# A transformer tower in one kernel: attention's input normalised inside the dense experts, query and key maxima from an unpadded product, attention three steps behind, switch-expert weights split earlier

## Chip, cores and metric

The kernel runs on one core of one Trainium2 chip. The metric is the device time of one execution in microseconds (us). Several executions are timed and their median is given. One further execution is recorded by the hardware profiler, and all rows below come from that one. TensorE is PE in the rows, its weight loads are PEld, VectorE is DVE, ScalarE is ACT, GpSimd is POOL, and SyncE's DMA queue is SPq.

## What is computed

The input is x of 16 x 2048 tokens of width 192 (D). A score keeps some of the tokens. Then four blocks follow, each adding to the stream h:

```python
h = _L0_tok_ref(x, ...)
h = h + _L0_attn_ref(_layernorm(h), ...)     # a state space scan
h = h + _L0_ffn_ref(_layernorm(h), ...)      # 16 dense experts and a shared one
h = h + _L1_attn_ref(_layernorm(h), ...)     # attention, 12 heads of 16, 8-bit fake_quant
h = h + _L1_ffn_ref(_layernorm(h), ...)      # 16 switch experts, 64 slots each in a batch
```

What matters here is the third line from below and the next one. `fake_quant` needs the largest absolute value of a whole tensor before it can round any of it:

```python
def fake_quant(x, n_bits=N_BITS):
    scale = jnp.maximum(jnp.max(jnp.abs(x)) / qmax, 1e-08)
    q = jnp.clip(jnp.round(x / scale), -qmax - 1, qmax) * scale
qkv = jnp.einsum('bnc,oc->bno', fake_quant(x), fake_quant(w_qkv)) + b_qkv
attn = jnp.einsum('bhnd,bhmd->bhnm', fake_quant(q), fake_quant(k)) * scale
out = jnp.einsum('bhnm,bhmd->bhnd', fake_quant(softmax(attn)), fake_quant(v))
out = jnp.einsum('bnc,oc->bno', fake_quant(out), fake_quant(w_proj)) + b_proj
```

So attention's input, q, k, v and its output each force a pass that only finds a maximum, with a result of one number for the whole chip, before the pass that uses it.

## The kernel before

The program is a row of stages. Every stage is a block of its own with buffers of its own; a block ends when all engines and its stores are done, so nothing overlaps across a seam. Names of buffers begin with the letter of their stage.

- a (token selection) and b (state space scan) are not touched.
- cw loads the dense experts' weights in five pieces; ACT writes the high part of each (line 842) and DVE the low part (line 849).
- c, in `dense_experts`, runs over NC = 20 chunks of 420 rows (four tiles of 105). A chunk has 17 slots e, one for an expert. In each slot PE makes up and gate products (`c_pU`, `c_pG`, lines 1032 to 1034), ACT the silu `c_su` (1118), DVE `c_pG` (1246) and `c_ac` (1253), ACT the high part `c_ap` (1121), POOL the low part (976), and PE the down product `c_pD` (1041). DVE fits the next chunk's routing into slots 4 to 12 and a row statistic into slots 0, 1, 2 and 12 (`STAT_AT`); ACT normalises in slots 13 to 16. At the end of a chunk `finish` adds `c_pD` to `c_y` (line 1223) and SP stores `c_y` (924) as h2.
- d, the first part of `attention_inputs`, loads h2 again, 16 batches of 525 rows (five tiles of 105), takes row statistics on DVE (1284 to 1292), normalises on ACT (1394), takes the maximum (1421, 1423) and stores `xn`. Behind the batches it quantises and transposes the attention weights (1430 to 1470) and lays them out with each head of 16 padded to 32 rows (`wT`).
- e loads xn by batch, rounds it (1606, 1610), transposes it (PE 1547, ACT 1584 to `e_xT`), multiplies it with the padded weights in six groups of 128 columns (PE 1560), copies each group out on ACT (`e_y`, 1591) and takes its maximum on DVE (1619), then v in two groups (PE 1567, DVE `e_vb` 1628) with its maximum (1637) and three small steps that merge the maxima (1640 to 1643). No q or k is kept; only the maxima, v and the transposed input are.
- f makes q and k once more, now scaled and rounded. g finds the softmax's row maxima and sums. It also fills the switch experts' slot table with zeros (`dram_slots`, line 1855, 16 DMAs of `k_empty`), which n later scatters into.
- h multiplies the probabilities with v. A batch has TN = 17 steps n of three 128 x 512 tiles. PE fills `h_pS` for step n+1 (`fill`, 2101, 2105); ACT takes the exponent into `h_ex` (2189); DVE rounds it into `h_pr` (2260); PE combines it with v into `h_pO` (`combine`, 2119, 2122), two steps behind. `h_ex`, `h_pr` and `h_pS` have two buffers, `h_pO` one. After the last tile of each of three groups of heads (steps 5, 11 and 16) DVE copies `h_pO` out (`evacuate`, 2228, at DVE's n = 7, 13 and 1 of the next batch) before PE may write the next group; `largest` (2237, 2239) takes its maximum.
- i is the output projection. n is the router, which scatters rows into slots (POOL, 2504).
- o, in `switch_experts`, runs 16 experts, each with four chunks of 256 slots: PE transposes (2773, 2774), `o_pH` (2789 to 2791) and `o_pY` (2800, 2803). The weights of the next expert are split while the current one runs: high parts on ACT (2828 to 2830), low parts on POOL (2864, 2865) and a narrow rest on DVE (2906). POOL also scatters the results (`out_dram`, 2875, two for each chunk, waiting for DVE's `o_yr`).

The order of instructions on each engine is the order in which the code is written. An engine runs its own list in order and waits at a semaphore; `at(b, n, d)` is the count after b rounds of n signals and d more.

## Time and profile before

| | us |
|---|---|
| median of three runs | 4838.54 |
| lowest and highest | 4837.43, 4840.34 |
| the profiled execution | 4844.94 |
| its span | 4843.2 |
| c, first product's wait to last result | 1194 to 2418.65 |
| d, first load to last copy | 2422.96 to 2547.1 |
| e | 2548.07 to about 2724 |
| f | about 2728 to 2827 |
| g | 2833 to 3419.8 |
| h | 3421.38 to 3929.3 |
| i | 3931.82 to about 4049 |
| n | 4051.70 to about 4280 |
| o | 4283.33 to the end |

The profiled execution took 4844.94 us, of which 4843.2 are its span. A group's row names the line, the engine, the operation, what it writes and reads, and how many instructions stand together; times are the start and the length. In square brackets stands how long the engine had been idle and what released it. Between about 1 and 10 us pass at each seam in which no engine computes.

### The profile page before, as it was taken

Reading aid. Unit: us, or ns where it says so; the run is one execution under the profiler, and the core shown is the slowest. Engines: PE = TensorE matmul, PEld = TensorE weight load, DVE = VectorE, ACT = ScalarE, POOL = GpSimd, SP = SyncE. Lnnn points to the kernel's source line nnn. Section 1 sums busy time; section 2 is a strip of 40 time slices with the busy share of each in tenths; the row PEclk is TensorE's granted clock in tenths of the full one; section 3 lists DMA queues with packets and bytes.
Section 4 is the critical chain, followed back from the end, with each engine's and each line's share of the span. In section 5 each row is a group of like instructions: output and inputs, shape, how many; then the busy total and the mean of one; then the engine's idle time right before and its main releaser. Section 6 shows DMA issues by size and latency. Waiting matters only on the chain. (4 is left out here: it accounts for less than half of the span.)

```text
span 4843.2 us, 75411 instructions
## 1 busy us (share of the span) xinstructions
PE 3765.6 (78%) x23732; PEld 2846.5 (59%) x23732; DVE 3528.1 (73%) x6651; ACT 2607.0 (54%) x5078; POOL 1768.2 (37%) x2215
## 2 busy tenths in 40 slices
PE   0059999995899999999907778888788853559998
PEld 0049999994799999999904421111122223459998
DVE  6849888986666666666477669999677755856665
ACT  4535555553344444444334579999788842433332
POOL 4647777773244444433300012222100012433333
PEclk9999999997899999999955655555555555579999
DMA  3235555444222222222233590000111145443332
GB/s 96 84 90 149 140 135 147 138 134 117 78 78 78 78 78 78 78 78 76 75 112 91 169 343 30 22 22 23 63 67 67 66 133 143 126 123 95 116 117 69
DMA packets 285815, 484.45 MB, mean 100 GB/s; under 512 B 47214, under 2 KB 217134, under 8 KB 272594
## 3 DMA queue, kind: packets, MB, share of 16 engines
q1 hardware_dynamic: 264082, 455.22, 30.4%
q0 software_dynamic: 20480, 25.87, 1.8%
q8 instruction: 115, 1.88, 0.2%
q14 instruction: 114, 0.93, 0.1%
q10 hardware_dynamic: 1024, 0.54, 0.0%
HBM read 354.05 MB, written 136.51 MB: 101 GB/s over the span
## 5 line engine op out<-in xcount | busy, mean ns | idle before, releaser
L976 POOL TENSOR_TENSOR c_ap<-c_ac,c_ap 128x420 fp32r<-128x420 f32 x340 | 428.6, 1261 | 733.9 <-ACT c_ap L1121 733.5
L693 PE MATMUL b_pA<-b_woutT,b_ys 128*105 128x192 f32 x3840 | 689.4, 326 | 1.3 <-ACT b_ho L579 0.4
L693 PEld LDWEIGHTS b_pA<-b_woutT,b_ys 128*105 128x105 f32 x3840 | 610.5, 171 | 12.1 <-ACT b_ho L579 3.9
L491 POOL TENSOR_TENSOR b_ys<-b_hs,b_cb 128x525 f32<-128x525 f32 x384 | 507.4, 1322 | 221.1 <-DVE b_hs L776 178.2
L1953 DVE TENSOR_REDUCE g_raw<-g_pS 128x1 f32<-128x525 f32 x816 | 549.5, 703 | 31.0 <-PE g_pS L1908 29.7
L1929 ACT ACTIVATE g_pS<-g_pS,g_stt 128x525 f32<-128x525 f32 x816 | 553.7, 776 | 19.3 <-POOL g_stt L1882 18.5
L1908 PE MATMUL g_pS<-g_qk 16*128 16x262 bf16 (+1 forms) x1536 | 461.4, 408 | 93.2 <-ACT g_pS L1929 35.7
L776 DVE TENSOR_TENSOR_SCAN b_hs<-b_ae,b_pB 128x525 f32<-128x525 f32 x384 | 479.1, 1248 | 39.8 <-ACT b_ae L606 5.1
L1121 ACT ACTIVATE c_ap<-c_ac 128x420 fp32r<-128x420 f32 x340 | 189.2, 557 | 589.9 <-DVE c_ac L1253 588.2
L1246 DVE SCALAR_TENSOR_TENSOR c_pG<-c_pG,c_bc,c_su 128x420 f32<-128x420 f32 x340 | 225.5, 663 | 325.1 <-ACT c_su L1118 316.8
L1041 PE MATMUL c_pD<-cw_wd,c_ap 128*105 128x192 f32 x4080 | 438.6, 257 | 18.6 <-POOL c_ap L976 18.6
L1041 PEld LDWEIGHTS c_pD<-cw_wd,c_ap 128*105 128x105 f32 x4080 | 424.3, 172 | 42.5 <-POOL c_ap L976 29.5
L2189 ACT ACTIVATE h_ex<-h_pS 128x1536 f32<-128x1536 f32 x272 | 385.3, 1451 | 85.2 <-DVE h_pr L2260 70.0
L1908 PEld LDWEIGHTS g_pS<-g_qk 16*128 16x128 bf16 x1536 | 95.5, 106 | 459.2 <-ACT g_pS L1929 425.9
L2260 DVE TENSOR_SCALAR h_pr<-h_ex 128x1536 bf16<-128x1536 f32 x272 | 257.6, 961 | 102.2 <-PE h_pO L2119 59.0
L606 ACT ACTIVATE b_ae<-b_delta,b_nlam 128x525 f32<-128x525 f32 x384 | 270.6, 727 | 82.0 <-DVE b_hs L776 79.6
L1882 POOL TENSOR_TENSOR g_stt<-g_raw,k_cs 128x1 f32<-128x1 f32 x816 | 155.9, 191 | 405.4 <-DVE g_raw L1953 405.4
L1032 PE MATMUL c_pU<-c_xp,cw_wu 128*128 128x420 f32 x1020 | 269.2, 372 | 28.3 <-DVE c_ac L1253 28.3
L767 DVE TENSOR_TENSOR b_pB<-b_delta,b_pB 128x525 f32<-128x525 f32 x384 | 265.3, 691 | 31.1 <-PE b_pB L683 29.2
L1929 ACT ACTIVATION_READ_ACCUMULATOR g_pS<-g_pS,g_stt 128x1 f32 x816 | 253.7, 311 | 0.0
L2875 POOL DMA_INDIRECT out_dram<-o_yr,o_xr x128 | 125.0, 977 | 346.6 <-DVE o_yr L2929 325.2
L1032 PE MATMUL c_pG<-c_xp,cw_wg 128*128 128x420 f32 x1020 | 250.7, 354 | 0.0
(385 smaller groups left out, 8366.6 us busy)
## 6 DMA issues: line engine op xcount, KB each, us to landing
b_cb<-dram_ct SPq DMA_DIRECT2D x64, 1050.0 KB
c_wb<-dram_wt SPq DMA_DIRECT2D x60, 840.0 KB, 10.5
b_cb<-dram_ct SPq DMA_DIRECT2D x64, 525.0 KB
dram_slots<-k_empty SPq DMA_DIRECT2D x16, 1544.0 KB
...
```

Source lines behind the costliest of these rows:

```text
L491: pool.tensor_tensor(ys[:, u % RING, :], hs[:, u % RING, :], cb[:, g % 3, u % GU, :], ALU.mult).then_inc(s["ys"], 1)
L606: act.activation(ae[:, u % RING, :], delta[:, k, q, :], ACT.Exp, scale=nlam[:, u:u + 1])\
L693: ins = pe.matmul(into, ys[:, u % RING, t * TP:(t + 1) * TP], woutT[:, u % NU, :], start=(u == 0 and t % 2 == 0), stop=(u % NU == NU - 1), ...
L767: v.tensor_tensor(pB[:, u % 2, OFF:OFF + S], delta[:, k, 0 if u < NS else 1, :], pB[:, u % 2, OFF:OFF + S], ALU.mult).then_inc(s["bm"], 1)
L776: v.tensor_tensor_scan(hs[:, u % RING, :], ae[:, u % RING, :], pB[:, u % 2, OFF:OFF + S], 0.0, ALU.mult, ALU.add).then_inc(s["hs"], 1)
L976: nc.gpsimd.tensor_tensor(ap[LO][:, r, :], ac[:, r, :], ap[HI][:, r, :].bitcast(F32), ALU.subtract)\
L1032: pe.matmul(into, ws[b][:, e, :], xp[a][:, k, 0, :], start=(n == 0), stop=False)
L1041: ins = pe.matmul(pD[:, t // 2, (t % 2) * D:(t % 2 + 1) * D], ap[a][:, (e + k) % 2, t * TP:(t + 1) * TP], wd_s[b][:, e, :], start=False, s ...
L1908: ins = pe.matmul(pS[:, slot, OFF + lo:OFF + hi], mine, qk[at_, k, 3 + g, lo:hi], start=True, stop=True)
L1929: nc.scalar.activation(x, x, ACT.Exp, bias=stt[:, k, 0, c:c + 1], scale=cs, accum_out=stt[:, k, 1, c:c + 1]).then_inc(s["exp"], 1)
L1953: v.tensor_reduce(raw[:, k, c:c + 1], pS[:, q % RING, OFF:OFF + S], AX, ALU.max, negate=True)\
L2189: nc.scalar.activation(ex[:, (n + k) % 2, :], pS[:, (n + k) % 2, :, :].rearrange("p t l -> p (t l)"), ACT.Exp, scale=cs).then_inc(s["E"], 1)
```

## The change

Five parts.

1. Stage d is gone. Its weight work (maxima, rounding, 18 transposes, copies, bias loads) now stands in the cw block, between the five `low_part` steps of DVE, with one more layout without padding (`wcT`) and its bias (`bc`). Its work on rows is in c: statistics of the finished chunk c-1 on DVE in slots 3, 13, 14 and 15, the normalisation of chunk c-2 on ACT in slots 6 to 9, its maximum on DVE in slot 16, and a second store (`store_normed`) on SP. `c_y` has three buffers. What is left of chunks 18 and 19, and the global maximum, follow the last chunk.
2. Stage e multiplies with the unpadded weights: three groups instead of six, so 12 products instead of 24, three copies and three maxima. Maxima of a batch go to columns of `e_mq` and `e_mv` and are merged once at the end. PE transposes the next batch ahead of v. It is written out for all batches, with three buffers of `e_y`.
3. The zero fill of the slot table is made from a buffer of half the size in g itself: 32 DMAs of 772 KB instead of 16 of 1544 KB, behind a wait for POOL's memset.
4. Stage h combines three steps behind, with three `h_ex` and four `h_pr`; DVE copies out at n = 8, 14 and 2; `largest` writes a column of `h_om`, and one reduction ends the stage. It is written out.
5. The first switch expert's weights are loaded at the start of n and split at its end. In o, POOL makes the low parts of the next expert's weights before it waits for the chunk's `o_yr`, no longer after its two scatters.

```diff
+    OSTAT_AT, OLN_AT, OMAX_AT = {3: 0, 13: 1, 14: 2, 15: 3}, {6: 0, 7: 1, 8: 2, 9: 3}, 16
...
+            sp.dma_start(wq_n[:, :, :], w_qkv.rearrange("(r p) c -> p r c", p=KC)).then_inc(s_wq, 16)
+            sp.dma_start(wp_n[:, :, :], w_proj.rearrange("(r p) c -> p r c", p=KC)).then_inc(s_wq, 16)
...
+            dve.wait_ge(s_wq, 32)
+            v.tensor_reduce(K["amax"][0:KC, 1:2], wq_n[:, :, :].rearrange("p r c -> p (r c)"), AX, ALU.max,
+                            apply_absolute_value=True).then_inc(s_m0, 1)
+            v.tensor_reduce(K["amax"][0:KC, 2:3], wp_n[:, :, :].rearrange("p r c -> p (r c)"), AX, ALU.max,
+                            apply_absolute_value=True).then_inc(s_m0, 1)
+            low_part(0)
+            st = Steps(dve, s_v2)
+            dve.wait_ge(s_all, 1)
+            quant_scale(nc, st, K["sc"][:, 1:3], K["inv"][:, 1:3], K["gmax"][:, 1:3])
...
+            dve.sem_inc(s_tc, 1)
+            low_part(1)
+            for c in range(KT):
+                dve.wait_ge(s_t, c + 1)
+                for r in range(4):
+                    v.tensor_copy(K["wT"][:, c, r * 6 * HP:(r + 1) * 6 * HP].rearrange("p (h d) -> p h d", d=HP)[:, :, 0:HD],
+                                  pT[0:KC, c, r * KC:(r + 1) * KC].rearrange("p (h d) -> p h d", d=HD))
+                v.tensor_copy(K["wcT"][:, c, :], pT[0:KC, c, 0:4 * KC])
+                ins = v.tensor_copy(K["wvT"][:, c, :], pT[0:KC, c, 4 * KC:6 * KC])
+            ins.then_inc(s_tc, 1)
+            low_part(2)
+            dve.wait_ge(s_t, 3)
...
+            def store_normed(c):
+                sp.wait_ge(s["zn"], at(c, 1, 1))
+                sp.dma_start(xn_d[c * CT:(c + 1) * CT, :, :].rearrange("t p d -> p t d"), z[:, c % 2, :, :])\
+                    .then_inc(s_z[c % 2], 16)
 
             def body(c, i, k, last):
                 rows(c + 3)
-                sp.wait_ge(s_out[k], i * 16)
-                sp.dma_start(y[:, k, :, :], tiles(h1, c)).then_inc(s_y[k], 16)
+                if c >= YR:
+                    sp.wait_ge(s_out[c % YR], c // YR * 16)
+                    sp.wait_ge(s["zn"], at(c - YR, 1, 1))
+                sp.dma_start(y[:, c % YR, :, :], tiles(h1, c)).then_inc(s_y[c % YR], 16)
                 if last < 2:
                     weights(c + 1, range(len(GROUPS)))
-                store(c, k)
+                if c >= 2:
+                    store_normed(c - 2)
+                store(c)
 
...
+        def normalise_result(c, t):
+            act = nc.scalar
+            if t == 0:
+                act.wait_ge(s["ostat"], at(c, 1, 1))
+                act.wait_ge(s["zm"], at(c, 1, -1))
+                act.wait_ge(s_z[c % 2], c // 2 * 16)
+            ins = act.activation(z[:, c % 2, t, :], y[:, c % YR, t, :], ACT.Identity, bias=nb2[:, t:t + 1],
+                                 scale=rs2[:, t:t + 1])
+            if t == CT - 1:
+                ins.then_inc(s["zn"], 1)
...
+                    if c >= 1:
+                        if e == min(OSTAT_AT):
+                            so = Steps(dve, s_vo, VP, c - 1)
+                        if e in OSTAT_AT:
+                            result_statistics(c - 1, OSTAT_AT[e], so)
+                    if c >= 2 and e == OMAX_AT:
+                        result_largest(c - 2)
                 finish(c, i, k)
 
             written_out(NC, body)
...
+            so = Steps(dve, s_vo, VP, NC - 1)
+            for part in range(4):
+                result_statistics(NC - 1, part, so)
+            for c in (NC - 2, NC - 1):
+                result_largest(c)
+            dve.wait_ge(s["zm"], at(NC - 1, 1, 1))
+            v.tensor_reduce(K["amax"][0:TP, 0:1], zm[:, :], AX, ALU.max).then_inc(s_m0, 1)
+            dve.wait_ge(s_all, 1)
...
+                for r in range(3):
+                    pe.wait_ge(s["y"], at(b, 3, r - 2))
+                    if r < 2:
+                        pe.wait_ge(s["vb"], at(b, 2, r - 1))
+                    for lo, hi in CUT:
+                        for c in range(KT):
+                            ins = pe.matmul(pQ[:, r, OFF + lo:OFF + hi], K["wcT"][:, c, r * 128:(r + 1) * 128],
+                                            xT[:, k, c, lo:hi], start=(c == 0), stop=(c == KT - 1))
+                    ins.then_inc(s["qk"], 1)
+                if last < 2:
+                    transposes(b + 1, 1 - k)
+                for r, (lo, hi) in enumerate(KV):
+                    pe.wait_ge(s["y"], at(b, 3, r + 1))
...
+            def body(b, i, k, last):
+                for r in range(3):
+                    act.wait_ge(s["qk"], at(b, 3, r + 1))
+                    act.wait_ge(s["max"], at(b, 3, r - 2))
+                    nc.scalar.activation(y[:, r, :], pQ[:, r, OFF:OFF + S], ACT.Identity,
+                                         bias=K["bc"][:, r:r + 1], scale=K["cq"][:, 0:1]).then_inc(s["y"], 1)
+                if last < 2:
+                    columns(b + 1, i + k, 1 - k)
+
...
+                for r in range(3):
+                    dve.wait_ge(s["y"], at(b, 3, r + 1))
+                    v.tensor_reduce(mq[:, r, b:b + 1], y[:, r, :], AX, ALU.max,
+                                    apply_absolute_value=True).then_inc(s["max"], 1)
+                dve.wait_ge(s_o2[k], i * 16)
+                dve.wait_ge(s["vmax"], at(b, 1, -1))
+                if last == 0:
+                    integers(b + 2, i + 1, k)
+                for r, (lo, hi) in enumerate(KV):
...
-SW, ER = 2 * D + 2, 8
+SW, ER = 2 * D + 2, 4
...
+            sp.wait_ge(s_i, 6)
...
-        ex = sb("ex", [128, 2, 3 * QM])
-        pr = sb("pr", [128, 2, 3 * QM], BF16)
+        BEHIND, EXR, PRR = 3, 3, 4
+        ex = sb("ex", [128, EXR, 3 * QM])
+        pr = sb("pr", [128, PRR, 3 * QM], BF16)
...
-        om = sb("om", [128, 1])
+        om = sb("om", [128, NB * HG])
...
-                    if n >= 2:
-                        combine(b, i, k, n - 2)
+                    if n >= BEHIND:
+                        combine(b, i, k, n - BEHIND)
                     elif not first:
-                        combine(b - 1, i + k - 1, 1 - k, TN + n - 2)
...
-                    act.wait_ge(s["P"], at(b, TN, n - 1))
-                    nc.scalar.activation(ex[:, (n + k) % 2, :], pS[:, (n + k) % 2, :, :].rearrange("p t l -> p (t l)"),
+                    act.wait_ge(s["P"], at(b, TN, n + 1 - EXR))
...
-                v.tensor_reduce(om[:, :], oT[:, k, g, :], AX, ALU.max, apply_absolute_value=True).then_inc(s_om, 1)
-                dve.wait_ge(s_om, b * HG + (g + 1))
-                v.tensor_tensor(K["amax"][:, 7:8], K["amax"][:, 7:8], om[:, :], ALU.max).then_inc(s["om"], 1)
-                dve.wait_ge(s["om"], at(b, HG, g + 1))
+                c = b * HG + g
+                v.tensor_reduce(om[:, c:c + 1], oT[:, k, g, :], AX, ALU.max, apply_absolute_value=True)\
+                    .then_inc(s["om"], 1)
...
-                    if n == 1 and not first:
+                    if n == BEHIND - 1 and not first:
                         evacuate(b - 1, i + k - 1, 1 - k, 2)
-                    if n in (7, 13):
-                        evacuate(b, i, k, 0 if n == 7 else 1)
+                    if n in (5 + BEHIND, 11 + BEHIND):
+                        evacuate(b, i, k, 0 if n == 5 + BEHIND else 1)
                     dve.wait_ge(s["E"], at(b, TN, n + 1))
-                    wait_combined(dve, b, n - 2)
-                    v.tensor_scalar(pr[:, (n + k) % 2, :], ex[:, (n + k) % 2, :], MAGIC, -MAGIC, ALU.add, ALU.add)\
+                    if n >= PRR or not first:
+                        wait_combined(dve, b, n - PRR)
+                    v.tensor_scalar(pr[:, (b * TN + n) % PRR, :], ex[:, (b * TN + n) % EXR, :], MAGIC, -MAGIC, ALU.add,
...
+                load_weights(sp, 0)
...
+                low_parts(pool, 0, 0)
...
+                high_parts(act, 0, 0)
...
-                split_weights(0, 0)
 
                 def body(c, i, j, last):
+                    if j % CE == 1 and not (last and j > CE):
+                        low_parts(pool, i * 2 + (j // CE + 1), 1 - j // CE)
                     pool.wait_ge(s["y"], at(c, 1, 1))
                     pool.sem_inc(s_go, 1)
                     for t in range(CT):
                         pool.indirect_dma_start(out.rearrange("b s d -> (b s) d"), bass.IndirectOffsetOnAxis(
                             ap=xr[:, j, t, PT:PT + 1].bitcast(U32), axis=0), yr[:, j % 4, t, :], None,
                             bounds_check=last_row, oob_is_err=False).then_inc(s_y[j % 4], 16)
-                    if j % CE == 1 and not (last and j > CE):
-                        split_weights(i * 2 + (j // CE + 1), 1 - j // CE)
 ```

DVE in e, one batch near the end of the stage. `k_amax` and `e_mt` merge the maxima. Before:

```order
L1619 TENSOR_REDUCE e_mtq<-e_y 128x1 x3
L1606 TENSOR_SCALAR e_xr<-e_x,k_inv 105x960
L1610 TENSOR_SCALAR e_xb<-e_xr 105x960
L1619 TENSOR_REDUCE e_mtq<-e_y 128x1 x3
L1628 SCALAR_TENSOR_TENSOR e_vb<-e_pQ,k_cq,k_bv 105x384 x2
L1628 SCALAR_TENSOR_TENSOR e_vb<-e_pQ,k_cq,k_bv 105x192
L1637 TENSOR_REDUCE e_mt<-e_vb 105x1
L1640 TENSOR_REDUCE e_mt<-e_mtq 128x2
L1642 TENSOR_TENSOR k_amax<-k_amax,e_mt 128x2
L1643 TENSOR_TENSOR k_amax<-k_amax,e_mt 105x1
```

And the same engine and place after the change:

```order
L1613 TENSOR_REDUCE e_mq<-e_y 128x1 x3
L1601 TENSOR_SCALAR e_xr<-e_x,k_inv 105x960
L1605 TENSOR_SCALAR e_xb<-e_xr 105x960
L1624 SCALAR_TENSOR_TENSOR e_vb<-e_pQ,k_cq,k_bv 105x384 x2
L1624 SCALAR_TENSOR_TENSOR e_vb<-e_pQ,k_cq,k_bv 105x192
L1630 TENSOR_REDUCE e_mv<-e_vb 105x1
```

Three reductions of a group and the three merging steps are gone from each batch.

DVE in h around the copy-out of the second group of heads (`h_oT<-h_pO`). Before:

```order
L2260 TENSOR_SCALAR h_pr<-h_ex 128x1536 x3
L2232 COPY h_oT<-h_pR 128x13
L2228 COPY h_oT<-h_pO 128x512
L2260 TENSOR_SCALAR h_pr<-h_ex 128x1536 x2
L2222 TENSOR_TENSOR h_qk<-h_qk,h_pR 128x525
```

And after:

```order
L2270 TENSOR_SCALAR h_pr<-h_ex 128x1536 x3
L2242 COPY h_oT<-h_pR 128x13
L2270 TENSOR_SCALAR h_pr<-h_ex 128x1536
L2236 COPY h_oT<-h_pO 128x512
L2270 TENSOR_SCALAR h_pr<-h_ex 128x1536
L2230 TENSOR_TENSOR h_qk<-h_qk,h_pR 128x525
```

The copy-out stands one rounding step later.

POOL in o, at the second chunk of an expert. Before:

```order
L2875 DMA out_dram<-o_yr,o_xr 8400x192 x2
L2863 ISA
L2864 TENSOR_TENSOR o_wi<-o_wi_r,o_wi 128x768
L2865 TENSOR_TENSOR o_wo<-o_wo_r,o_wo 128x6x192
L2872 REGISTER_ALU
L2875 DMA out_dram<-o_yr,o_xr 8400x192 x2
```

And after:

```order
L2899 DMA out_dram<-o_yr,o_xr 8400x192 x2
L2456 ISA
L2457 TENSOR_TENSOR m_wi<-m_wi_r,m_wi 128x768
L2458 TENSOR_TENSOR m_wo<-m_wo_r,m_wo 128x6x192
L2896 REGISTER_ALU
L2899 DMA out_dram<-o_yr,o_xr 8400x192 x2
```

The rows read alike, but the scatters above the two splits are those of the second chunk before and those of the first chunk after, since a scatter pair has moved from above to below.

## Rows read from the trace of the kernel before

**Rows 1.** Windows: stretch, its length, busy us (instructions) by engine, PEclk, DMA share, GB/s

```profile
1500.00:1600.00 100.00, 95.61 (x681) 91.36 (x680) 71.85 (x134) 41.50 (x77) 42.00 (x34) 1.00 0.23 78
...
2548.00:2724.00 176.00, 140.92 (x704) 83.37 (x704) 132.88 (x238) 93.45 (x128) 0.00 (x0) 0.50 0.31 90
...
3535.00:3635.00 100.00, 84.89 (x626) 22.71 (x626) 75.73 (x128) 80.64 (x67) 2.81 (x6) 0.50 0.20 69
```

**Rows 2.** Timeline at the seams from c to d to e: start, length, instruction

```profile
2417.63 1.02 DVE L1223 TENSOR_TENSOR c_y<-c_pD,c_y 105x384 f32<-105x384 f32 x2 [3.18 <-PE c_pD L1041]
...
2422.96 0.32 SPq L1336 DMA_DIRECT2D d_wq_n<-in_L_attn_w_qkv_dram  x1
...
2548.07 4.91 SPq L1508 DMA_DIRECT2D e_x<-dram_xn  x3
```

**Rows 3.** Timeline of DVE, the first row statistic of stage c

```profile
1200.80 1.14 DVE L1141 BATCH_NORM_STATS2 c_stats<-c_h 105x6 f32<-105x192 f32 x4 [7.13 <-DMA c_bd_s<-in_L_ffn_sbd_dram]
...
1204.88 0.16 DVE L1157 SCALAR_TENSOR_TENSOR c_nb<-c_mv,c_rs 105x4 f32<-105x4 f32 x1
```

**Rows 4.** Timeline of ACT in the weight block cw

```profile
1182.23 2.02 ACT L842 ACTIVATE cw_wgt<-cw_raw 128x2176 fp32r<-128x2176 f32 x1 [3.17 <-DMA cw_raw<-in_L_ffn_sWg_dram]
```

**Rows 5.** Stage c: timeline of DVE; then waits of 1500:2300 (us in total, times, longest)

```profile
1603.85 1.06 DVE L1150 TENSOR_SCALAR c_rs<-c_hh 105x4 int32<-105x4 int32 x1
...
PE c_pU L1032 <- DVE c_ac L1253: 17.9, 29, 1.0
```

**Rows 6.** Timeline of ACT, PE and DVE over one batch of stage e

```profile
2575.75 1.10 ACT L1584 ACTIVATE e_xT<-e_pT 96x525 bf16<-96x525 bf16 x2 [1.96 <-PE e_pT L1547]
...
2586.19 1.10 ACT L1584 ACTIVATE e_xT<-e_pT 96x525 bf16<-96x525 bf16 x2 [1.63 <-PE e_pT L1547]
...
2577.08 5.97 PE L1560 MATMUL e_pQ<-e_xT,k_wT 96*128 96x263 bf16 x24 [1.52 <-ACT e_xT L1584]
...
2579.08 0.70 DVE L1619 TENSOR_REDUCE e_mtq<-e_y 128x1 f32<-128x525 f32 x1 [1.28 <-ACT e_y L1591]
...
2585.20 1.46 DVE L1628 SCALAR_TENSOR_TENSOR e_vb<-e_pQ,k_cq,k_bv 105x384 f32<-105x384 f32 x3
2586.81 1.15 DVE L1637 TENSOR_REDUCE e_mt<-e_vb 105x1 f32<-105x960 f32 x1 [0.15 <-DVE e_vb L1628]
```

**Rows 7.** Stage h: timeline of POOL, once a batch; then waits of 3480:3900

```profile
3621.54 0.45 POOL L1794 TENSOR_TENSOR h_kt<-h_qk,h_mask 128x156 bf16<-128x156 bf16 x1 [4.07 <-DMA h_qk<-dram_qk]
...
3652.21 0.46 POOL L1794 TENSOR_TENSOR h_kt<-h_qk,h_mask 128x156 bf16<-128x156 bf16 x1 [4.01 <-DMA h_qk<-dram_qk]
...
ACT h_ex L2189 <- DVE h_pr L2260: 61.4, 81, 1.6
...
DVE h_pr L2260 <- PE h_pO L2119: 50.9, 67, 1.1
...
PE h_pO L2119 <- DVE h_oT L2228: 34.7, 42, 1.1
```

**Rows 8.** Timeline of ACT and POOL at the start of stage o

```profile
4292.97 0.84 ACT L2828 ACTIVATE o_wi<-o_wi_r 128x768 fp32r<-128x768 f32 x1 [30.16 <-DMA o_wo_r<-in_L_ffn_wo_dram]
...
4298.21 2.61 POOL L2865 TENSOR_TENSOR o_wo<-o_wo_r,o_wo 128x1152 fp32r<-128x1152 f32 x1
```

**Rows 9.** Timeline of DVE, ACT and PE around an expert's first product in o

```profile
4295.63 0.95 DVE L2906 TENSOR_TENSOR o_wi_t<-o_wi_r,o_wi_t 64x768 fp32r<-64x768 f32 x1 [27.42 <-ACT o_wo L2830]
...
4393.63 4.61 DVE L2906 TENSOR_TENSOR o_wi_t<-o_wi_r,o_wi_t 64x768 fp32r<-64x768 f32 x1
...
4386.81 1.16 ACT L2830 ACTIVATE o_wo<-o_wo_r 128x1152 fp32r<-128x1152 f32 x1
...
4398.44 0.61 PE L2789 MATMUL o_pH<-o_xT,o_wi 128*128 128x256 f32 x3 [2.35 <-issue]
...
4399.28 0.84 PE L2789 MATMUL o_pH<-o_xT,o_wi 128*128 128x256 f32 x3
...
4403.01 0.52 PE L2789 MATMUL o_pH<-o_xT,o_wi 128*128 128x256 f32 x3
```

## What the change was expected to do

> **What bounds the kernel now.** The stages run one after the other, so each has to be read alone. First the busy time by windows [rows 1]. In c PE is busy 95.61 of 100 us at full clock, DVE 71.85. In e PE is busy 140.92 of 176 us and DVE 132.88, at clock 0.50: two engines that hand work to each other. In h PE is busy 84.89 of 100 us, ACT 80.64, DVE 75.73, at 0.50: nobody is full. Then the timeline at the seams, which shows d as a stage in which PE has nearly nothing to do [rows 2]. Then the waits and timelines of e, h and o, for what ends the idle time there. The sum is made against the profiled execution's 4844.94 us; the median of the three runs is 4838.54, 6.4 us less, and I take these 6.4 off at the end.
>
> **Stage d goes.** The last result of c is written at 2417.63 + 1.02 = 2418.65, and e's first load is issued at 2548.07 [rows 2]: 129.4 us. After the change this stretch holds only a tail. Statistics of the last chunk cost what they cost at the start of c, where DVE is alone: 1200.80 to 1205.04 [rows 3], 4.2 us. Four ACT normalisations of 105x192 come next; I estimate 2 us. The maximum over 105x768 is about 768/960 of the 1.15 us reduction of 105x960 [rows 6], 0.9 us, but runs beside the store's flight. From c's last result to the first load of d, store and seam took 2422.96 - 2418.65 = 4.3 us [rows 2]; the same comes behind the store of the normalised rows, with about 1.5 us for the last reduction, the one over partitions and the scale. 4.2 + 2 + 4.3 + 1.5 = 12 us. **Saved: 117**, bounds 110 to 121.
>
> **The weight work in cw.** DVE gets about 8 us more in five gaps, and ACT and DVE wait there for DMA: 3.17 us before the fourth piece [rows 4]. Most fits. The two new loads (576 KB) stand first in the queue and push the pieces back; the fourth wait shows that a piece arrives every 5.2 us for 1.1 MB, so about 2.7 us. **+3**, bounds 1 and 8.
>
> **The row work in c.** Each chunk gets on DVE the 4.2 us of a statistic [rows 3], and 0.9 of a maximum; on ACT four normalisations; on SP one wait and one store behind the next chunk's weights and ahead of the store of h2. 20 x 5.1 = 102 us of DVE work lie beside PE, since DVE is idle 28 of 100 us [rows 1], 16 in a chunk of about 59, and the slots chosen carry no routing. What it costs is delay, not work. Small DVE steps are sometimes held while POOL runs: a step on a few elements took 0.16 us alone [rows 3] and 1.06 here [rows 5]. This is the place to weigh a rule: the Trainium skill, page "SBUF — State Buffer", section "SBUF: two separate sides", says that POOL and a DVE instruction with two SBUF inputs or in a fast mode take one pair of ports as an exclusive lock, and the later one waits for the whole other instruction. The rows agree in kind; by that rule all new steps may each be held, and also hold POOL's `c_ap`.
> PE waits for `c_ac` at each chunk's start, 17.9 us in 29 waits over 800 us [rows 5], so a late DVE at the end of slot 16 goes straight to PE. The new maximum stands just there. Slots 13 to 16 get about 1.2 us each where, at 16 us in 17 slots, they have some 1 to 2 us idle. I take 0.3 us a chunk: **+6**, bounds 0 and 24 (1.2 us a chunk, one held step that nothing absorbs). If the cover were gone altogether it would be 102.
>
> **Stage e.** A batch takes 2586.19 - 2575.75 = 10.44 us [rows 6]: 24 products in 5.97 us, then v, while ACT and DVE follow with six copies and six maxima. PE's busy time a batch is 140.92 / 16 = 8.8 us, less twelve products of 0.25: 5.8. DVE's is 132.88 / 16 = 8.3 [rows 1], less three maxima of 0.70 and three merging steps of 0.16: 5.7. The loop that closes runs from `e_vb` to the first maximum of the next batch, since `e_pQ` is shared: from the first product to that maximum it was 2579.08 - 2577.08 = 2.0 us [rows 6], plus 0.2 for the signal. DVE has the rest of `e_vb` (0.5) and the maximum of v (1.15) to do in it, so 0.6 is idle; its steps that follow each other with a wait cost some 0.8 more. 5.7 + 0.6 + 0.8 = 7.1. The transposes, ahead of v now, hide the 1.52 us in which PE waits for `e_xT` [rows 6]. 16 x (10.44 - 7.15) = **-52**, bounds -40 (8 us, if the loop shows one more wait) and -62 (6.6, DVE gapless).
>
> **Stages f and g.** f is not touched. In g the zero fill is the same bytes in twice the DMAs, now behind a memset; nobody reads the table until n. 0, bounds -8 and +3.
>
> **Stage h.** A batch takes 3652.21 - 3621.54 = 30.67 us [rows 7]. ACT waits for DVE's rounding (61.4 us in 81 waits over 420 us, 13.7 batches), DVE for PE's `combine` (50.9 in 67), PE for the copy-out (34.7 in 42) [rows 7]. The first two are buffers: `h_ex` and `h_pr` have two each. With three and four, and a combine one step later, both go. The third stays, for `h_pO` still has one buffer: three times 0.8 us a batch. Then PE is next: 84.89% of 30.67 is 26.0 us [rows 1], plus 3 x 0.8 = 2.4, is 28.4; ACT needs 80.64%, 24.7. DVE loses 48 merging steps. Saved 2.3 x 16 = 37, and a little in the written-out loop. **-38**, bounds -15 (the steps around each copy-out still drain two engines) and -50 (the copy-out partly hidden as well).
>
> **Start of o.** The first weights reach ACT at 4292.97, and POOL ends its split at 4298.21 + 2.61 = 4300.82, when PE may start [rows 8]. Now they are split already and PE needs only its rows: some 10 us less. Against it POOL's 5.2 us of splits stand behind n's last scatters and may hold the seam. **-8**, bounds -11 and 0.
>
> **The stalls in o.** At each new expert PE waits 2.35 us [rows 9]; the row says "issue", but the start, 4398.44, follows the end of DVE's step 2906 at 4398.24, which took 4.61 us where the first of its kind took 0.95 [rows 9]. It was held while POOL split the same weights. After the change POOL splits right after ACT's high parts, which ended at 4386.81 + 1.16 = 4387.97 [rows 9], and POOL's two splits take twice 2.6 us [rows 8], so until about 4393.2. DVE's step at 4393.63 is then free and done at 4394.6, before PE needs it at 4398.44 - 2.35 = 4396.1. 15 experts after the first: 15 x 2.3 = 34. Behind each stall PE runs at half clock: groups of three products take 0.84 us where they later take 0.52 [rows 9], four groups of 1.0 in place of 0.59, 1.6 us lost, x15 = 24. I take 21 of it. **-55**, bounds -27 and -60.
>
> Sum: -117 + 3 + 6 - 52 + 0 - 38 - 8 - 55 = -261. 4844.94 - 261 = 4583.9 profiled, 4577.5 as the median.
>
> **Rivals.**
> 1. h stays coupled: around the copy-out PE, DVE and ACT drain as now, and the longer buffers only move the waits. For it: 42 PE waits on the copy-out are untouched, and it is one DVE step later. Against: two of the three waits are plain buffer waits. Gain 15 in place of 38: 4600.5.
> 2. The clock rises in h and e. h would have fewer gaps on PE than now, and c, which has few, runs at 2.4 GHz where h runs at 1.2 [rows 1]. ACT then bounds h at 24.7 + 0.3: 3.4 x 16 = 54 more, and e goes to 6.5, 10 more: 4513.5. Against: the three copy-outs a batch stay as gaps, and no stretch of h is above 0.50 so far. The Trainium skill, "TensorE: Matmul & The Clock Gate", Part 1, says that activity lifts the clock from 1.2 to 2.4 GHz; by it the rival is the likelier the fewer gaps are left. h's row at 0.50 shows only how it is with the gaps of now [rows 1].
> 3. The stall in o only moves: POOL's splits are slowed by DVE, end after 4393.6, and DVE's step is held by the second of them or by the scatters. Half of the 55 stays: 4604.5.
> 4. c pays 1.2 us a chunk, +24 in place of +6: 4595.5.
> 5. e does not shorten as walked (the 8 us batch, and v's wait for ACT's copies ahead of it): +14 to +25: 4597.
> 6. **The slower side**, one mechanism: in c the held small steps delay `c_ac` in slots 13 to 16, POOL's `c_ap` follows late, PE empties, and the delay repeats in each chunk. It decides from (261 + 6) / 20 = 13.4 us a chunk, over a fifth of one: with 14 the median is 4577.5 + 20 x 14 - 6 = 4851.5. DVE's idle 16 us in a chunk against 5.1 speak against it.
> That the change does nothing is no case: d's loads and batches are gone from the program.
>
> **How the numbers follow.** Forecast 0.50; rival 1 0.13; rival 2 0.11; rival 3 0.12; rival 4 0.08; rival 5 0.04; rival 6 and failures like it 0.02. The forecast's own bounds add to about 4565 to 4595. For 8 in 10 the range takes in rivals 1, 3, 4 and 5, two of them together, and the clock rising in e alone or for a part of h: 4540 to 4622. About 0.2% (9.7 us) is what a measurement can tell: faster by more 0.975, within 0.010, slower 0.015, all from rival 6 and its approach.
>
> **What would show it.** c ends where it did, within 10 us, plus 3 for cw. From c's last `c_y` to e's first load 12 us. e's `e_xT` every 7.1 us. h's `h_kt` every 28.4 us, with no wait of DVE for PE's combine and PE's waits on `h_oT` left. In o no idle before an expert's first product, DVE's narrow step at 0.95 us, and PE's clock at 1.00. Wrong would be: `c_pU` waiting over 2 us for `c_ac`, a clock other than 0.50 in h, or a DVE step of over 2 us in o.

## The result and the profile after

The kernel before took 4839.44 in four runs beside it (4837.43 to 4843.04). The ratio is 0.9523, with a 95% interval of 0.9506 to 0.9539. The forecast was 4577.5, with a range of 4540 to 4622. So the sign and the range hold, and the gain of 231 us is 30 less than the 261 that the sum gave. The kernels of the experiments below ran once each, except the last one (`best`). Their stage times come from that one profile, so a difference is held against the spread of stages whose code is the same; the last section lists it.

The profiled execution took 4606.7 us, of a span of 4605.0. The stages, each from its first DMA issue to that of the next one, in us:

| stage | before | after | difference | forecast |
|---|---|---|---|---|
| cw, c, d (to e's first load) | 1387.1 | 1283.1 | -104.0 | -108 |
| e | 180.3 | 142.2 | -38.1 | -52 |
| f | 105.2 | 103.1 | -2.1 | 0 |
| g | 587.9 | 587.9 | 0.0 | 0 |
| h | 510.4 | 476.3 | -34.1 | -38 |
| i | 119.9 | 120.6 | +0.7 | 0 |
| n | 231.6 | 238.3 | +6.7 | with o |
| o | 559.9 | 492.9 | -67.0 | -63 with n |

In the profiled executions the difference is 4844.94 - 4606.7 = 238.2 us, against 261. The windows of the changed kernel answer to [rows 1]; the columns are the same:

```profile
1500.00:1600.00 100.00, 94.53 (x679) 90.40 (x678) 79.06 (x168) 47.48 (x87) 41.93 (x33) 1.00 0.18 61
...
2452.00:2575.00 123.00, 76.43 (x478) 61.35 (x476) 87.22 (x132) 51.97 (x75) 0.00 (x0) 0.59 0.41 114
...
3400.00:3500.00 100.00, 85.14 (x649) 24.33 (x659) 79.77 (x130) 84.24 (x71) 6.91 (x8) 0.50 0.22 76
...
4200.00:4300.00 100.00, 100.00 (x785) 100.00 (x784) 60.48 (x113) 40.44 (x65) 45.77 (x36) 1.00 0.36 109
```

In o's window PE is never idle now and its clock is 1.00. In h the busy share of PE is as it was, 85%, over shorter batches. In e PE is busy 76.43 of 123 us, 62%, where it was 80% [rows 1]: it does less work and waits more.

The seam from c to e, which answers to [rows 2], in the timeline of DVE and SP:

```profile
2431.92 1.02 DVE L1382 TENSOR_TENSOR c_y<-c_pD,c_y 105x384 f32<-105x384 f32 x2 [1.66 <-PE c_pD L1154]
...
2433.35 5.99 SPq L1025 DMA_DIRECT2D dram_xn<-c_z  x2
2443.63 0.85 SPq L1494 DMA_DIRECT2D e_x<-dram_xn  x2
```

From 2432.94 to 2443.63 are 10.7 us in place of 129.4.

### The profile page after: what moved, and what is told of

Same layout as the page of the kernel before. It is cut to its first block and busy times, and to the rows that moved or that the text cites. A ratio compares the mean times of both kernels' runs of the same rounds, so it can differ in the third digit from the quotient of the medians.

```text
span 4605.0 us, 72550 instructions
## 1 busy us (share of the span) xinstructions
PE 3655.4 (79%) x23492; PEld 2806.7 (61%) x23540; DVE 3458.5 (75%) x6558; ACT 2558.1 (56%) x5030; POOL 1784.9 (39%) x2216
## 5 line engine op out<-in xcount | busy, mean ns | idle before, releaser
L1086 POOL TENSOR_TENSOR c_ap<-c_ac,c_ap 128x420 fp32r<-128x420 f32 x340 | 428.2, 1260 | 743.8 <-ACT c_ap L1245 743.4
L1154 PE MATMUL c_pD<-cw_wd,c_ap 128*105 128x192 f32 x4080 | 438.1, 257 | 27.5 <-POOL c_ap L1086 27.5
L1154 PEld LDWEIGHTS c_pD<-cw_wd,c_ap 128*105 128x105 f32 x4080 | 423.6, 172 | 51.5 <-POOL c_ap L1086 38.4
L2197 ACT ACTIVATE h_ex<-h_pS 128x1536 f32<-128x1536 f32 x272 | 374.7, 1465 | 48.9 <-PE h_pS L2109 27.5
L1405 DVE SCALAR_TENSOR_TENSOR c_pG<-c_pG,c_bc,c_su 128x420 f32<-128x420 f32 x340 | 225.4, 663 | 228.0 <-ACT c_su L1242 218.6
L2270 DVE TENSOR_SCALAR h_pr<-h_ex 128x1536 bf16<-128x1536 f32 x272 | 259.1, 962 | 68.7 <-ACT h_ex L2197 56.2
L1145 PE MATMUL c_pU<-c_xp,cw_wu 128*128 128x420 f32 x1020 | 268.4, 371 | 30.4 <-DVE c_ac L1412 30.4
L1145 PE MATMUL c_pG<-c_xp,cw_wg 128*128 128x420 f32 x1020 | 251.3, 355 | 0.0
L2899 POOL DMA_INDIRECT out_dram<-o_yr,o_xr x128 | 132.1, 1032 | 261.3 <-DVE o_yr L2945 237.7
```

What stands on the lines that cost most here:

```text
L1086: nc.gpsimd.tensor_tensor(ap[LO][:, r, :], ac[:, r, :], ap[HI][:, r, :].bitcast(F32), ALU.subtract)\
L1145: pe.matmul(into, ws[b][:, e, :], xp[a][:, k, 0, :], start=(n == 0), stop=False)
L1154: ins = pe.matmul(pD[:, t // 2, (t % 2) * D:(t % 2 + 1) * D], ap[a][:, (e + k) % 2, t * TP:(t + 1) * TP], wd_s[b][:, e, :], start=False, s ...
L2197: nc.scalar.activation(ex[:, (b * TN + n) % EXR, :], pS[:, (n + k) % 2, :, :].rearrange("p t l -> p (t l)"), ACT.Exp, scale=cs).then_inc(s ...
```

## Stage e: where the largest miss was

The waits of e in the changed kernel (us in total, times, longest; 2450 to 2580), and one batch in the timeline of SP, DVE and PE:

```profile
PE e_pQ L1548 <- DVE e_vb L1624: 46.8, 15, 4.3
DVE e_xr L1601 <- DMA e_x<-dram_xn: 20.6, 13, 2.4
...
2483.69 0.35 SPq L1494 DMA_DIRECT2D e_x<-dram_xn  x1
...
2489.52 0.72 DVE L1601 TENSOR_SCALAR e_xr<-e_x,k_inv 105x960 f32<-105x960 f32 x1 [2.19 <-DMA e_x<-dram_xn]
...
2490.85 1.46 DVE L1624 SCALAR_TENSOR_TENSOR e_vb<-e_pQ,k_cq,k_bv 105x384 f32<-105x384 f32 x3
...
2492.13 2.79 PE L1548 MATMUL e_pQ<-e_xT,k_wcT 96*128 96x263 bf16 x12 [3.96 <-DVE e_vb L1624]
```

The load of `e_x` is issued at 2483.69 and DVE can round it only at 2489.52, 5.8 us later. DVE waits 2.19 us for it, with `e_vb` queued behind, and PE waits 3.96 us for `e_vb`. A batch takes 8.2 to 9.4 us where the walk gave 7.15. The theory: SP issues the load too late. Its buffer is free long before, but on SP it stands behind the store of v of the batch before, which waits for `e_vb`. The rival: the loop over `e_vb`, product, copy and maximum takes 8 us by itself.

**Load one batch earlier** (e_load).

```diff
-            for k in range(2):
-                load(k, 0, k)
+            for b in range(3):
+                load(b, b // 2, b % 2)
...
-                if not last:
-                    load(b + 2, i + 1, k)
+                if b + 3 < NB:
+                    load(b + 3, (b + 3) // 2, (b + 3) % 2)
```

> The changed kernel with SP issuing the load of e_x three batches ahead of the batch in work in place of two; buffers stay two. Theory (load late): e missed its forecast because DVE waits for e_x (20.6 us in 13 waits) with e_vb queued behind the rounding, and PE waits for e_vb. The wait goes, a batch takes 7.1 to 7.4 us where it takes 8.2 to 9.1, and e goes from 142 to 126 to 129 us. Rival (loop): the loop over e_vb, product, copy and maximum takes 8 us by itself; then DVE's wait for DMA moves to another wait and e stays over 138 us.

Measured: e 120.4 us in place of 142.2, the execution 4585.67. PE and DVE of that kernel:

```profile
2491.52 2.79 PE L1548 MATMUL e_pQ<-e_xT,k_wcT 96*128 96x263 bf16 x12 [1.60 <-DVE e_vb L1624]
...
2498.39 2.79 PE L1548 MATMUL e_pQ<-e_xT,k_wcT 96*128 96x263 bf16 x12 [1.59 <-DVE e_vb L1624]
...
2495.78 0.71 DVE L1601 TENSOR_SCALAR e_xr<-e_x,k_inv 105x960 f32<-105x960 f32 x1
```

The batch is 6.87 us and DVE's rounding waits for nothing. The load was the cause; e came out below the 126 to 129 us that were expected, so the rest of the walk was even a little too long.

**Rounding behind `e_vb`** (e_ints): the two steps of `integers(b + 2)` on DVE follow the maximum of v; the loads are issued as in the change.

```diff
-                if last == 0:
-                    integers(b + 2, i + 1, k)
                 for r, (lo, hi) in enumerate(KV):
...
                                 apply_absolute_value=True).then_inc(s["vmax"], 1)
+                if last == 0:
+                    integers(b + 2, i + 1, k)
```

> The changed kernel with DVE's rounding of batch b+2 (integers) behind e_vb and the maximum of v, in place of ahead of e_vb; loads as in the change. Theory (load late): e_vb no longer stands behind the wait for e_x, so PE's wait for e_vb (46.8 us in 15) falls under 20 us and e takes 126 to 133 us. Rival (loop): e stays over 138 us.

Measured: e 117.3 us, the execution 4586.13, with c 3 us longer in that run. It confirms the same from the other side: the loads are issued where they were, but the rounding comes later, finds its data and no longer stands in front of `e_vb`. e is 25 us shorter, again below the expectation, and a batch takes 6.57 us, less than the 6.87 of the early load. PE's rows tell where the 0.3 us are: the wait for `e_vb` is 1.10 us in place of 1.60.

```profile
2498.49 2.79 PE L1548 MATMUL e_pQ<-e_xT,k_wcT 96*128 96x263 bf16 x12 [1.10 <-DVE e_vb L1622]
```

What the halved products, the copies and the order of the transposes are worth one by one was not measured.

## Stage h: which of the three loosenings counts

In the changed kernel `h_kt` follows after 28.3 us in the two rows shown (POOL, answering to [rows 7]); twelve batches in the middle take 28.6 us in the mean, 26.6 to 30.1 each, where before they took 30.5. Among the waits of 3340 to 3700 DVE's for PE has nearly gone, and PE's for the copy-out has grown to 40.2 / 38 = 1.06 us each:

```profile
3407.30 0.45 POOL L1801 TENSOR_TENSOR h_kt<-h_qk,h_mask 128x156 bf16<-128x156 bf16 x1 [3.72 <-DMA h_qk<-dram_qk]
...
3435.64 0.46 POOL L1801 TENSOR_TENSOR h_kt<-h_qk,h_mask 128x156 bf16<-128x156 bf16 x1 [3.37 <-DMA h_qk<-dram_qk]
...
PE h_pO L2127 <- DVE h_oT L2236: 40.2, 38, 1.3
...
ACT h_ex L2197 <- PE h_pS L2109: 16.8, 25, 1.1
...
DVE h_pr L2270 <- PE h_pO L2127: 9.9, 26, 0.4
```

Three things were loosened together, and the maxima and the loop were changed too. All five runs edit the changed kernel. Four of them change only the numbers of this line (the copy-outs follow BEHIND), shown for h_lag2; h_om puts back the three lines of the maxima instead.

```diff
-        BEHIND, EXR, PRR = 3, 3, 4
+        BEHIND, EXR, PRR = 2, 3, 4
```

> The changed kernel with h combining two steps behind again (copy-outs at DVE n = 7, 13, 1), while h_ex keeps three and h_pr four buffers. Theory (buffers): the waits of ACT and DVE were for buffers, so most of h's gain stays: a batch takes 28.6 to 29.3 us (28.6 with the change, 30.7 before). Rival (lag): PE must be a step later for its rounding to be ready, and the batch goes back to 30 us or more, with PE waiting for h_pr.

> The changed kernel with two h_ex buffers in place of three; three steps behind and four h_pr stay. If ACT's wait for DVE (61.4 us over 420 before) was what the gain of h came from, it returns and a batch takes 29.5 to 30.7 us. If the gain is the lag and the buffers of h_pr, a batch stays at 28.6 to 29.0 us.

With a lag of two (2, 3, 4) h takes 475.0 us; with two `h_ex` (3, 2, 4) 476.3; the change has 476.3. Kernels with the same code of h spread over 2.1 us, so neither of the two is shown to be worth anything while the others stay. So everything was undone (2, 2, 2), and apart from that the maxima:

> The changed kernel with h two steps behind and two buffers each of h_ex and h_pr, so all of the looser order undone; the columns of maxima and the written-out order stay. h took 510.4 us before and 476.3 with the change; with either the lag or the third h_ex alone undone it took 475.0 and 476.3. Theory (h_pr): the number of h_pr buffers is what frees DVE and ACT; then h goes to 500 us or more. Rival (maxima): the gain is the 48 merging steps with their waits between DVE and itself; then h stays under 482 us.

> The changed kernel with only the maxima of h undone: one column, a TENSOR_TENSOR and two waits of DVE after each of 48 reductions, as before. Rival (maxima): h goes to 500 us or more. Theory (h_pr): 48 steps of about 0.4 us mostly hidden, h stays under 484 us.

Measured: (2, 2, 2) gives 501.7, the maxima undone alone 476.7. So 25.4 of the 34.1 us come from the three, and the 0.4 of the maxima, while the buffers are there, is inside the spread. The waits of (2, 2, 2), 3330 to 3700, are those of before again:

```profile
ACT h_ex L2197 <- DVE h_pr L2270: 48.3, 62, 1.6
...
DVE h_pr L2270 <- PE h_pO L2127: 44.3, 50, 1.1
```

Since each of two could stand in for the other, the last run keeps four `h_pr` and nothing else (2, 2, 4):

> The changed kernel with h two steps behind and two h_ex buffers as before; only h_pr keeps four. With all three undone h took 501.7 us, with the change 476.3; the lag alone undone gave 475.0, the third h_ex alone 476.3. Theory (h_pr alone): the copy-out of h_pO holds combine, and only more rounded tiles let DVE and ACT go on meanwhile; h stays under 480 us. Rival (any two): each of the lag and the third h_ex can stand in for the other, and one is needed; then h is 488 us or more.

Measured: 474.8 us. The execution took 4617.56, with the stages ahead of h longer than in the change. Here are the waits of that kernel, 3330 to 3700:

```profile
DVE h_pr L2270 <- ACT h_ex L2197: 48.9, 78, 0.9
...
PE h_pO L2127 <- DVE h_oT L2236: 32.9, 39, 1.1
...
ACT h_ex L2197 <- DVE h_pr L2270: 18.0, 13, 1.6
...
DVE h_pr L2270 <- PE h_pO L2127: 9.9, 26, 0.4
```

Two more buffers of `h_pr` are enough for all of it. The chain before was: PE waits for the copy-out of `h_pO`; so no `combine` frees an `h_pr`; DVE waits for that; so no `h_ex` comes free; ACT waits for that. With four `h_pr` DVE goes on rounding over the copy-out, and ACT waits for a free `h_ex` only once a batch (13 waits in 370 us, where (2, 2, 2) has 62). Whether a third `h_ex` with two `h_pr` would do the same was not run: four `h_pr` are shown to be enough, not to be the only cure. What remains open are 510.4 - 501.7 = 8.7 us: the order written out and the maxima, both still changed in (2, 2, 2), were not separated there.

## Stage c: half a microsecond in a chunk

A chunk took 59.20 us in the middle before and 59.89 after; from the first `c_y` to the last it was 1116.7 and is 1128.6. PE's waits, 1500 to 2300, show that the wait for POOL grew from 12.5 us and the one for `c_ac` [rows 5] hardly did; the DVE steps of the last chunk show why:

```profile
PE c_pD L1154 <- POOL c_ap L1086: 19.1, 27, 1.4
PE c_pU L1145 <- DVE c_ac L1412: 18.8, 28, 1.0
...
2423.05 1.05 DVE L1303 TENSOR_SCALAR c_rs<-c_hh 105x4 int32<-105x4 int32 x1
...
2426.14 1.08 DVE L1320 SCALAR_TENSOR_TENSOR c_hh<-c_hh,c_ve 105x4 f32<-105x4 f32 x1
...
2427.45 0.66 DVE L1405 SCALAR_TENSOR_TENSOR c_pG<-c_pG,c_bc,c_su 128x420 f32<-128x420 f32 x1
```

In slots 13 and 14 one small step each takes about 1 us in place of 0.16, and the next `c_pG` starts with no idle time before it, so DVE is late. Of the 13 new small steps of a chunk these two are the only ones held, and POOL's `c_ap` takes 1.27 us in the mean before and after. So the case that the prediction weighed, every new step held and `c_ap` with them, did not come. By offsets from `c_y` (mean of 12 chunks, against before), `c_ac` falls back by 0.44 us over slot 14. Theory: the two Newton steps of slot 14. Rival: the maximum in slot 16.

**One Newton step a slot** (c_newton):

```diff
-    OSTAT_AT, OLN_AT, OMAX_AT = {3: 0, 13: 1, 14: 2, 15: 3}, {6: 0, 7: 1, 8: 2, 9: 3}, 16
+    OSTAT_AT, OLN_AT, OMAX_AT = {3: 0, 13: 1, 14: 2, 15: 3, 16: 4}, {6: 0, 7: 1, 8: 2, 9: 3}, 16
...
-            elif part == 2:
-                newton(st, y_, v_, h_)
+            elif part < 4:
                 newton(st, y_, v_, h_)
```

> The changed kernel with the three Newton steps of the result's statistics spread over slots 14, 15 and 16 of c, one each, in place of two in slot 14 and one in 15; the maximum stays in slot 16. A chunk takes 59.9 us with the change and 59.2 before; PE's added wait is for c_ap at a chunk's end. Theory (slot 14): six small steps, one of them held while POOL runs, make DVE late in slot 14; spread, a chunk takes 59.3 to 59.6 and c is 5 to 11 us shorter. Rival (maximum): the maximum in slot 16 is what delays; no change, within 2 us.

**The maximum in slot 3 of the next chunk** (c_max3):

```diff
-                    if c >= 2 and e == OMAX_AT:
-                        result_largest(c - 2)
+                    if c >= 3 and e == OMAX_AT:
+                        result_largest(c - 3)
```

> The changed kernel with the maximum of the normalised rows moved from slot 16 to slot 3 of the next chunk. Theory (slot 14): no change of c, within 2 us. Rival (maximum): a chunk takes 59.3 to 59.6 us and c is 5 to 11 us shorter.

| | first to last `c_y` | middle chunk | `c_pD` waits for POOL, 1500:2300 |
|---|---|---|---|
| before | 1116.7 | 59.20 | 12.5 |
| change | 1128.6 | 59.89 | 19.1 |
| c_newton | 1125.5 | 59.68 | 14.0 |
| c_max3 | 1127.2 | 59.78 | 19.1 |
| both (in `best`) | 1120.3 | 59.36 | 14.0 |

Nine other kernels with c as in the change have 1128.6 to 1129.9, so 3 us is a difference and 1.4 is little more than their spread. Slot 14 is shown as the cause of PE's longer wait for POOL. Neither expectation of 5 to 11 us came: in c_newton one step fewer is held in a chunk, but the step that moved lands in front of the maximum in slot 16, and 0.25 us are lost there. With the maximum away as well 8.3 of the 11.9 us come back, more than the 3.1 and 1.4 of the two moves alone. So the theory and the rival each held a part of the cause, and 3.6 us stay open.

## Stage o, and the end of n

**The order of POOL undone** (o_order):

```diff
-                    if j % CE == 1 and not (last and j > CE):
-                        low_parts(pool, i * 2 + (j // CE + 1), 1 - j // CE)
                     pool.wait_ge(s["y"], at(c, 1, 1))
...
                             bounds_check=last_row, oob_is_err=False).then_inc(s_y[j % 4], 16)
+                    if j % CE == 1 and not (last and j > CE):
+                        low_parts(pool, i * 2 + (j // CE + 1), 1 - j // CE)
```

> The changed kernel with one part undone: in o POOL makes the low parts of the next expert's weights behind the second chunk's two scatters again, as before. Theory (order): the whole gain of o comes from this order. PE stalls about 2.3 us before each of 15 experts' first product, the DVE step on the narrow part (L2464) takes over 4 us in place of 0.95, PE runs at half clock after each stall, and o grows from 493 by 50 to 58 us. Rival (preload): the gain comes from the weights of the first expert and from loads that are issued earlier; then o grows by under 15 us.

Measured: 4669.08 us; o 549.9 in place of 492.9, so 57.0 us for this one order. PE's waits before the 15 first products sum to 34.6 us, which leaves 22.4; they are put down to PE's clock, as the windows further down show it. DVE and PE of that kernel, then POOL and DVE of the changed one at the same place:

```profile
4218.61 4.61 DVE L2464 TENSOR_TENSOR m_wi_t<-m_wi_r,m_wi_t 64x768 fp32r<-64x768 f32 x1
...
4223.43 0.62 PE L2825 MATMUL o_pH<-o_xT,m_wi 128*128 128x256 f32 x3 [2.35 <-issue]
```

```profile
4169.11 1.84 POOL L2457 TENSOR_TENSOR m_wi<-m_wi_r,m_wi 128x768 fp32r<-128x768 f32 x1 [2.52 <-ACT m_wo L2453]
4170.90 2.67 POOL L2458 TENSOR_TENSOR m_wo<-m_wo_r,m_wo 128x1152 fp32r<-128x1152 f32 x1
...
4174.68 0.95 DVE L2464 TENSOR_TENSOR m_wi_t<-m_wi_r,m_wi_t 64x768 fp32r<-64x768 f32 x1
```

POOL ends at 4173.57 and DVE's narrow step starts 1.1 us later and takes 0.95.

The half clock does not follow every stall. These are the windows of 4 us behind two of the stalls of o_order, after 2.35 and 2.29 us of idle time of PE; the clock is the third number from the end:

```profile
4223.40:4227.40 4.00, 3.98 (x33) 3.98 (x34) 3.30 (x7) 1.31 (x3) 1.50 (x2) 1.00 0.02 8
4255.70:4259.70 4.00, 4.00 (x21) 4.00 (x22) 2.53 (x6) 0.60 (x1) 1.59 (x2) 0.57 0.05 18
```

Behind 12 of the 15 stalls the mean clock of these 4 us is 0.57 to 0.69, behind three it is 1.00, and in the kernel before it is 12 and three as well. So a fall of the clock costs about 22.4 / 12 = 1.9 us. Why three stalls go without it no run shows.

The remaining 10 us of o (559.9 - 549.9) are the start. From o's first load to the first product are 4119.32 - 4112.07 = 7.25 us by the row below. Before it was 17.5: PE could start when POOL ended at 4300.82 [rows 8], and o began at 4283.33.

```profile
4119.32 0.99 PE L2825 MATMUL o_pH<-o_xT,m_wi 128*128 128x256 f32 x3
```

**Weights later in n** (n_late):

```diff
-                load_weights(sp, 0)
...
+                    if c == 2:
+                        load_weights(sp, 0)
                     if c:
```

> The changed kernel with the first switch expert's weights loaded in n behind the third batch's loads, in place of at n's start. Theory (loads in front): n's first statistic starts 1.3 us later than before (11.1 after 9.8 us) and n runs 4.2 us longer to its last scatter because 1.2 MB of weights stand among its first loads; both go, and from n's first load to o's first load it is 233 to 236 us in place of 238.1. Rival (end of n): all of the 6.7 us more are POOL's splits behind the last scatter; then it stays within 1 us of 238.

Measured: n 237.0 us, in place of 238.3, outside the 233 to 236 of the theory. The first statistic starts 9.6 us after the first load in place of 11.2. But kernels with n as in the change have 10.0 to 11.9 us there, and before had 10.0, so the weights' place is hardly shown in it. From the first to the last statistic it is 188.1 us as in the change (187.7), where before had 184.6. And c_newton, whose n is that of the change, had 184.5 and n 234.6. So these 3 us are not the weights' place; they come and go between executions of the same code, and what sets them stays open. What every execution shows is the end, 2.3 us of the 6.7: POOL's splits stand behind the last scatter, until

```profile
4101.96 2.63 POOL L2458 TENSOR_TENSOR m_wo<-m_wo_r,m_wo 128x1152 fp32r<-128x1152 f32 x1
```

and o's first load is at 4112.07, 11.9 us after the end of the last scatter, where it was 9.6.

## What the runs add up to

> The changed kernel with the load of e_x one batch earlier, the rounding behind e_vb, the Newton steps spread over slots 14 to 16, the maximum in slot 3 of the next chunk, and the weights of n loaded later. e alone gave 120.4 and 117.3 us for 142.2: I expect e at 115 to 118. In c the spread took 0.43 us off slot 14 and gave 0.26 back around slot 16, where the maximum stands; with the maximum away a chunk takes 59.35 to 59.5 us in place of 59.9, 7 to 10 us in all. n gives at most 2. Together 4570 to 4577 us. If the two moves in c do not add (the maximum only moves its delay to slot 3), 4578 to 4584.

Measured: 4572.32 us in the median of four runs (4570.80 to 4573.31), against 4840.65 for the kernel before in the same series; the ratio is 0.9445 (0.9429 to 0.9461). e takes 117.8 us, cw and c 1274.2, n 234.0. It is faster than both kernels, by 36 us than the change; the ratios' intervals, 0.9429 to 0.9461 and 0.9506 to 0.9539, lie apart. The two moves in c do more than add, by the table above. n's 234.0 is inside what n does from one execution to the next, and is not put down to the weights.

More of the change, by code:

```diff
@@ L1353, in turn @@
+                sp.wait_ge(s["vb"], at(b, 2, 2))
+                sp.sem_inc(s_gs, 1)
+                sp.dma_start(v_d[b], vb[:, k, :, :].rearrange("p t d -> p (t d)")).then_inc(s_o2[k], 16)
+            for k in range(2):
+                load(k, 0, k)
             def turn(b, i, k, last):
+                if not last:
+                    load(b + 2, i + 1, k)
                 store(b, k)
-                if not last:
-                    sp.dma_start(h[:, k, :, :], rows(h2, b + 2)).then_inc(s_h[k], 16)
+            written_out(NB, turn)
@@ new lines, in _, with body @@
+        @block.tensor
+        def _(pe):
+            pe.sem_inc(s["qk"], CREDIT)
+            def body(b, i, k, last):
+                pe.wait_ge(s_x[k], i * 32 + 32)
+                for r in range(6):
+                    pe.wait_ge(s["y"], at(b, 6, r - 2))
+                    for lo, hi in CUT:
+                        for c in range(KT):
+                            ins = pe.matmul(pQ[:, r % 3, OFF + lo:OFF + hi], K["wT"][:, c, r * 128:(r + 1) * 128],
+                                            xT[:, k, c, lo:hi], start=(c == 0), stop=(c == KT - 1))
+                    ins.then_inc(s["qk"], 1)
+            two_a_turn(pe, NB, body)
@@ L2743, in rows @@
                     sp.dma_start(xr[:, r, :, D:KB + SW], mine[:, :, KA:SW]).then_inc(s_x[r], 16)
-                rows(0, 0)
-                weights(0)
-                for r in range(1, AHEAD):
+                for r in range(AHEAD):
                     rows(r, r)
```

847 lines of the change are left out of this document (387 added, 460 removed).

## The prediction, step by step

Of the three signs of being wrong none came: `c_pU` waits at most 1.0 us for `c_ac`, h's clock is 0.50, and the longest narrow step of DVE in o is 0.96 us. Of the signs that would show it three came only in part: e took 8.2 to 9.4 us a batch for 7.1, DVE still waits 9.9 us in 360 for PE's combine in h, and c's last result came 14.3 us later, where 10 and the 3 of cw were allowed.

- **Stage d (-117)** was right: 129.4 - 10.7 = -118.7. The statistics and the normalisations came as estimated (4.2 and 1.86 us). What was shorter is the end: from the last normalisation to e's first load are 2443.63 - 2439.00 = 4.6 us, where the sum laid 1.5 for the last reductions and 4.3 for store and seam end to end. They ran side by side.

```profile
2437.14 1.86 ACT L1209 ACTIVATE c_z<-c_y,c_nb,c_rs 105x192 f32<-105x192 f32 x4 [5.84 <-DVE c_nb L1310]
```

- **cw (+3)** was a little low: the block and its seam took 1198.86 - 1160.50 = 38.4 us for 33.4, +4.9. The wait for the fourth piece was 4.23 us, where it was 3.17 [rows 4], and ACT starts on it 26.1 us after the block's first load, where it was 21.3. So the queue of loads still set the pace, and the new loads cost more than the 2.7 us that the sum took from their bytes:

```profile
1186.60 2.02 ACT L898 ACTIVATE cw_wgt<-cw_raw 128x2176 fp32r<-128x2176 f32 x1 [4.23 <-DMA cw_raw<-in_L_ffn_sWg_dram]
```

- **c (+6)** was low: 1234.1 for 1224.3, +9.8, inside its bounds. The mechanism, held small steps on DVE, was right, and 0.3 us a chunk was too small: it is 0.63. The place was half right. I put it at the maximum in slot 16 and at `c_ac`; the larger part sat in slot 14 and came to PE over POOL's `c_ap`, and the maximum counted only beside it.
- **e (-52)** is the step that failed: -38. The step "the loop that closes runs from `e_vb` to the first maximum of the next batch" looked at PE, ACT and DVE and left out SP. The rounding had moved two batches ahead and in front of `e_vb`, while its load still stood on SP behind a store that waits for `e_vb`. The bound of -40 was for "one more wait", and the measured -38 lies just outside it. With the load early the batch is 6.87 us and e 120.4, near the far bound of -62. So the engines' loop was well costed and the queue that feeds it was not looked at.
- **h (-38)** was right in size (-34). The reading "two of three waits are buffers" was right, but both waits were one, and two buffers of one tile cure it. A batch takes 28.6 us in the mean for the forecast 28.4, and before it took 30.5 in the mean where the one interval that I used had 30.67; these two make up the missing 4 us. The two terms of the 28.4 did not both hold. The copy-out costs PE 1.06 us each time in place of 0.8, and PE's busy time is 24.4 us a batch in place of 26.0, though its products are the same; 1.0 us are other waits. That this adds to nearly the forecast is partly luck. In h_pr4 they hold as forecast, 25.8 and three times 0.84.
- **o and n (-63)**: -60. The stalls and their half clock were -57 for -55. The stalls were right (34.6 for 34). The half clock was right in its sum (22.4 for 21) but not in its working: it follows 12 of the 15 stalls at 1.9 us, where I had all 15 at 1.6 and took something off, so that the sum fits is luck. POOL's second split took about the 2.6 us that I gave each, the first one 1.84. The start gave 10 as said, and n took 6.7 back where the forecast had left 2 for it.
- **The clock** did not rise in h: 0.50. In e it is 0.59 in the mean of the window, so for part of the time at the higher level. With the load early it is 0.53, and the batch is shorter:

```profile
2455.00:2555.00 100.00, 75.48 (x476) 60.77 (x475) 86.71 (x133) 50.67 (x75) 0.00 (x0) 0.53 0.48 137
```

The prediction took the rise to be the likelier the fewer gaps are left. The rows of e go the other way: PE was busy for 80% of the time before, at 0.50, for 75% with the load early, at 0.53, and for 62% in the change, at 0.59. What the partial rise was worth in e no run separates; e was longer than forecast and not the rival's 10 us shorter.
- **From profile to median.** I took 6.4 us off, since the profiled execution of before lay that far above its runs. For the changed kernel it lies 1.3 below. 7.7 of the 30.5 us of the miss are this. The sum's own error is 4606.7 - 4583.9 = 22.8: e 14, c and cw 6, h 4, n and o 3, i 1, less 2 each in the tail of d and in f, and rounding.

## What to carry to other kernels

When a step is pulled ahead on one engine, its load must be pulled ahead on the queue that issues it too, and a queue that runs in order may hold it behind a store that waits for another step. Where three waits stand in a ring, look for the one buffer that breaks it before loosening all: here two more `h_pr` gave all of the gain, and a longer lag and a third `h_ex` beside them added nothing. A long step of DVE beside POOL may be a hold and not work; moving POOL's work forward by one wait was worth 57 us here.
